# The order of the rows in W^T V, and who issues the first loads, in a fused low-rank FFN kernel

## The reference

```
base   = x @ W.T                                   # W: 1024 x 1024
logits = x @ Wr.T + 5.0 * one_hot(id)              # 8 experts
gates  = softmax over the top 2 of logits
h      = x @ A.T                                   # A: 8 experts x rank 16
lora   = (h * gates) @ B.T
out    = x + (base + 2.0 * lora) @ (U * S @ V.T).T # V: 1024 x 256, U: 1024 x 256
```

## Time and profile before

| | us |
|---|---|
| median of 3 runs | 157.66 |
| lowest, highest | 156.87, 158.06 |
| the profiled execution | 156.68 |
| its span, first to last instruction | 154.9 |
| busy TensorE, VectorE, ScalarE, GpSimd | 150.1, 103.1, 65.1, 70.1 |

### The profile page before, as it was taken

How to read it: one execution, slowest core, us unless ns; L and a number is a source line. 1 busy time by engine, 2 the same in 40 slices (tenths; PEclk the granted TensorE clock), 3 DMA queues, 4 the chain that set the end, 5 groups by cost and what they waited for, 6 DMA issues and landing times.

```text
span 154.9 us, 2559 instructions
## 1 busy us (share of the span) xinstructions
PE 150.1 (97%) x883; PEld 139.8 (90%) x883; DVE 103.1 (67%) x299; ACT 65.1 (42%) x147; POOL 70.1 (45%) x53
## 2 busy tenths in 40 slices
PE   7899999999999999999999999999999999999991
PEld 5799999999998999989998999899999989998880
DVE  0698697353658798765578476929692967396861
ACT  4696692519724642551155125414441642233200
POOL 2000024087764741259445935591669068701800
PEclk9999999999999999999999999999999999999999
DMA  5999999995303064148428744854680087006184
GB/s 184 326 395 395 405 418 405 408 402 204 135 7 130 4 271 135 80 154 310 136 99 312 268 135 180 287 215 135 261 259 25 0 292 252 2 22 253 70 333 141
DMA packets 10957, 32.72 MB, mean 211 GB/s; under 512 B 1472, under 2 KB 2496, under 8 KB 10816
## 3 DMA queue, kind: packets, MB, share of 16 engines
q1 hardware_dynamic: 10512, 31.96, 55.9%
q10 hardware_dynamic: 432, 0.59, 1.1%
HBM read 24.16 MB, written 8.39 MB: 210 GB/s over the span
## 4 chain that ended last, share of the span: by engine, by line
PE 93%; DMA 3%; DVE 1%; ACT 0%; ACTq 0%; issue 0%; DVEq 0%
PE pj L317 16%; PE pj L318 16%; PE pj L319 16%; PE fin L317 14%; PE fin L318 13%; PE fin L319 13%; DMA vw_raw<-in_VW 3%; PE zt L384 2%; PE gt L366 1%; PE zt L317 1%; PE zt L319 1%; PE zt L318 1%; DVE w_lo L702 0%; ACT w_hi L556 0%; DVE x_all L831 0%; ACTq L655 0%
## 5 line engine op out<-in xcount | busy, mean ns | idle before, releaser
L273 POOL TENSOR_TENSOR xT_lo<-xt_raw,xT_hi 128x1024 fp32r<-128x1024 f32 x16 | 40.5, 2532 | 55.1 <-ACT xT_hi L571 55.1
L317 PE MATMUL pj<-proj_hi,xT_hi 128*128 128x392 f32 x128 | 44.9, 351 | 0.0
L318 PE MATMUL pj<-proj_lo,xT_hi 128*128 128x392 f32 x128 | 43.5, 340 | 0.0
L319 PE MATMUL pj<-proj_hi,xT_lo 128*128 128x392 f32 x128 | 43.5, 340 | 0.0
L288 POOL TENSOR_TENSOR x_all<-x_all,vw_raw 128x512 f32<-128x512 f32 x18 | 23.0, 1295 | 17.5 <-DVE vw_raw L806 17.5
L317 PE MATMUL fin<-v_hi,w_hi 128*128 128x256 f32 (+1 forms) x84 | 26.9, 321 | 0.5 <-DVE w_lo L702 0.5
L318 PE MATMUL fin<-v_lo,w_hi 128*128 128x256 f32 (+1 forms) x84 | 26.3, 313 | 0.0
L319 PE MATMUL fin<-v_hi,w_lo 128*128 128x256 f32 (+1 forms) x84 | 26.3, 313 | 0.0
L317 PEld LDWEIGHTS pj<-proj_hi,xT_hi 128*128 128x128 f32 x128 | 24.0, 188 | 1.0
L318 PEld LDWEIGHTS pj<-proj_lo,xT_hi 128*128 128x128 f32 x128 | 24.1, 188 | 0.5
L319 PEld LDWEIGHTS pj<-proj_hi,xT_lo 128*128 128x128 f32 x128 | 24.0, 188 | 0.0
(11 more groups left out here) (87 smaller groups left out, 230.8 us busy)
## 6 DMA issues: line engine op xcount, KB each, us to landing
xt_raw<-in_xt SPq DMA_DIRECT2D x16, 512.0 KB, 3.6
x_all<-in_x SPq DMA_DIRECT2D x16, 512.0 KB, 5.7
out<-x_all SPq DMA_DIRECT2D x13, 512.0 KB, 2.7
w_raw<-in_W SPq DMA_DIRECT2D x8, 256.0 KB, 7.3
vw_raw<-in_VW SPq DMA_DIRECT2D x5, 384.0 KB, 6.8
out<-x_all SPq DMA_DIRECT2D x5, 256.0 KB, 2.0
u_raw<-in_U SPq DMA_DIRECT2D x1, 1024.0 KB, 13.0
vw_raw<-in_VW SPq DMA_DIRECT2D x3, 192.0 KB, 3.3
```

The lines of the kernel that those rows point to most:

```text
L273: nc.gpsimd.tensor_sub(xT_lo[:, t % 2, :, :], xt_raw[:, t % XTR, :, :], xT_hi[:, t % 2, :, :].bitcast(F32)).then_inc(xt_lo, 1)
L317: nc.tensor.matmul(dst, l_hi, r_hi, start=first, stop=False, skip_group_check=shared)
L318: nc.tensor.matmul(dst, l_hi, r_lo, start=False, stop=False, skip_group_check=shared)
L319: return nc.tensor.matmul(dst, l_lo, r_hi, start=False, stop=last, skip_group_check=shared)
```

## The change

The chunks of W^T V go by whole rows: chunk i is half h = i % 2 of row k = i // 2. V is split at every other chunk. SP issues both pieces of row 0, W[1], and then VW[k] and W[k] for k = 2 to 7, with ids, A|Wr, xt[0] and B between them. ScalarE issues nothing before its table load and its small exponential; after them it issues W[0] and VW[1]. The casts of A|Wr, x and B stand behind chunks 8, 10 and 12. All four banks become final in the last two chunks, and a new semaphore `p_ready` tells of them one by one; `split_p` for all four follows the last chunk. `step(0)` waits for one bank at every other k. TensorE makes 6 zero products instead of 7.

```diff
         def w_chunk(i):
-            return vw_raw[:, i, RANK:RANK + HQ] if i < OC else w_raw[:, i - OC, :]
+            return vw_raw[:, i // 2, RANK:RANK + HQ] if i % 2 == 0 else w_raw[:, i // 2, :]
...
             first = RANK + P
-            for k in range(3):
-                sp.dma_start(vw_raw[:, k, 0:first], VW[k, :, 0:first]).then_inc(vw_load[k], 16)
-            for k in range(3, OC):
+            sp.dma_start(vw_raw[:, 0, 0:first], VW[0, :, 0:first]).then_inc(vw_load[0], 16)
+            sp.dma_start(vw_raw[:, 0, first:], VW[0, :, first:]).then_inc(vw_rest_load, 16)
+            load_w(1)
+            for k in range(2, OC):
                 sp.dma_start(vw_raw[:, k, :], VW[k, :, :]).then_inc(vw_load[k], 16)
-            sp.dma_start(ids_i[:, :], ids).then_inc(ids_load, 16)
-            for k in range(OC):
                 load_w(k)
-            sp.dma_start(aw_raw[:, :, :], AW).then_inc(aw_load, 16)
-            load_xt(0)
-            sp.dma_start(b_raw[:, :, :], B).then_inc(b_load, 16)
+                if k == 2:
+                    sp.dma_start(ids_i[:, :], ids).then_inc(ids_load, 16)
+                if k == 4:
+                    sp.dma_start(aw_raw[:, :, :], AW).then_inc(aw_load, 16)
+                if k == 5:
+                    load_xt(0)
+                if k == 6:
+                    sp.dma_start(b_raw[:, :, :], B).then_inc(b_load, 16)
...
             def p_chunk(i):
-                h, k = divmod(i, OC)
+                k, h = divmod(i, 2)
...
+                    if k == OC - 1 and m % 2 == 1:
+                        last.then_inc(p_ready, 1)
+                if k < OC - 1:
+                    last.then_inc(w_used, 1)
...
                     if s == 0 and k == 0:
                         pe.wait_ge(aw_lo, 1)
-                        pe.wait_ge(p_lo, 2)
-                    if s == 0 and k in (MH, MH + 2):
+                    if s == 0 and k % 2 == 0:
                         pe.wait_ge(p_lo, k // 2 + 1)
...
-            for n in range(7):
+            for n in range(6):
...
             def split_p(b):
-                act.wait_ge(w_used, OC if b < 2 else 2 * OC)
+                act.wait_ge(p_ready, b + 1)
...
-            first = RANK + P
-            for k in range(3):
-                act.dma_start(vw_raw[:, k, first:], VW[k, :, first:]).then_inc(vw_rest_load[k], 16)
             act.wait_ge(const, 3 + E)
             nc.scalar.activation(esum[:, :], iota_e[:, 0:1], ACT.Exp).then_inc(act_warm, 1)
             act.wait_ge(act_warm, 1)
+            act.dma_start(w_raw[:, 0, :], W[0, :, :]).then_inc(w_load[0], 16)
+            act.dma_start(vw_raw[:, 1, :], VW[1, :, :]).then_inc(vw_load[1], 16)
             for i in range(2 * OC):
-                if i < OC:
-                    split_v(i)
+                if i % 2 == 0:
+                    split_v(i // 2)
                 split_w(i)
-                if i == OC + 4:
+                if i == OC:
                     act.wait_ge(aw_load, 16)
                     nc.scalar.copy(proj_hi[:, :, 0:Z0], aw_raw[:, :, :]).then_inc(aw_hi, 1)
-                if i == OC + 3:
-                    split_p(0)
-                    split_p(1)
-                if i == OC + 5:
+                if i == OC + 2:
                     split_x(0)
-                if i == OC + 6:
+                if i == OC + 4:
                     act.wait_ge(b_load, 16)
                     nc.scalar.copy(b_hi[:, :, :], b_raw[:, :, :]).then_inc(b_hi_done, 1)
-            split_p(2)
-            split_p(3)
+            for b in range(FINS):
+                split_p(b)
```

## The result

The changed kernel takes 160.37 us in the median of four runs (159.32 to 162.29), the kernel before 157.43; the ratio is 1.017, with a 95% interval of 1.012 to 1.022. A second set of runs gave 160.58 us and 1.020 (1.016 to 1.025). It is slower by 1.7 to 2.0%. The ratios leave out single runs that lie more than 1.5% above the fastest of their kernel, here the one of 162.29 us. The forecast was 158.6 us, 0.9 us up, with a chance of 0.66 for a change within 1% and 0.29 for slower by more than that.

The account below looks back on a forecast made before the run. The prediction took chunk 2's start, set by waits for the first loads, to bound the kernel. Its terms summed to +0.9 us, all at chunk 2, giving 158.6 us on the median, with a range of 156.8 to 160.4.

Parts of the forecast that it names:

- rival C: TensorE's clock stays or falls back low over chunks 1 and 2: +2.5 us, 160.2 us; chance 0.07.
- the main case: VW[1] lands late and delays chunk 2: +0.9 us, shift from -0.1 to +2.3, 157.5 to 160.0 us; chance 0.55.
- What sets the time: TensorE's start: no gap from chunk 2 at 8.57 us to step(0), so chunk 2's start sets the kernel's time.
- Issue times: ScalarE's queue: table load from 0.73 us, then W[0] issued at 2.27 and VW[1] at 2.7.
- Rival B: ScalarE's table load waits for iota_e until 1.9 us, both issues 1.2 us later: +2.1 us, 159.8 us; chance 0.08.
- Landing of W[0] and VW[1]: First loads: W[0] lands at 5.9 us, VW[1] at 7.8, within 6.7 to 9.1; chunk 2 at 9.5 instead of 8.57.
- the rate: First loads: bytes move at 375 GB/s, so the 1.84 MB taken for VW[1] are moved at 6.8 us.
- The equal share of the two queues: SP and ScalarE queues share the DMA engines about equally; middle counts 1.84 MB for VW[1], 1.12 MB for W[0].
- The lag: First loads: from bytes moved to landing takes 1.0 us, between 0.6 and 1.4.
- That W[0] decides nothing: Chunk 1 starts at 7.3 us and is over at 8.7, so VW[1] decides when chunk 2 starts.
- A zero product less: TensorE's start: chunk 0 at about 3.75 us instead of 4.14, worth 0.4 us there and nothing to chunk 2.
- A|Wr, x, B between chunks at no cost: Casts among the chunks cost 0 while the 1 us margin and stored chunks hold, even with a load 2 us later.

Follow-up runs that it names:

- e1_fill: Changed kernel with 14 products of zeros on TensorE between chunk 0 and chunk 1; 159.51 us, 1.012 of the kernel before.
- e1_again: The changed kernel with 14 zero products between chunks 0 and 1, run once more; 159.58 us, 1.014 of the kernel before.
- e3_act_first: Changed kernel with ScalarE's issues of W[0] and VW[1] ahead of its table load; 158.60 us, 1.004 of the kernel before.
- e7_before_6zeros: Kernel before with 6 zero products instead of 7 and nothing else; 157.40 us, 0.999 of the kernel before.
- e8_act_first_late: Changed kernel with ScalarE's two issues ahead of its table load, and A|Wr, x and B behind the rows; 158.46 us, 1.004 of the kernel before.
- e10_x_on_dve: Changed kernel, all loads on SP in use order, A|Wr behind row 5, x and B behind row 7, first x tile's low part on VectorE; 157.28 us, ratio 1.000.
- e2_sp_all: Changed kernel with W[0] and VW[1] issued by SP in order of use, ScalarE issuing nothing; 157.50 us, 0.9985 of the kernel before.
- e4_before_table: Kernel before with ScalarE's three pieces of rows 0 to 2 issued after its table load and small exponential; 162.50 us, 1.028 of the kernel before.
- a_again: The changed kernel itself, run once more; 160.58 us, 1.020 of the kernel before.
- e6_after_late: Changed kernel with loads and casts of A|Wr, x and B put back to the end of the rows; 161.87 us, 1.029 of the kernel before.
- e5_sp_all_late: Changed kernel with all loads on SP in use order, A|Wr, x, B loaded behind row 7, cast behind chunks 12 to 14; 157.37 us, ratio 1.000.

## Why the prediction was right or wrong

The measured 160.37 us lies at the upper edge of the range (160.4), and the likeliest time was 1.8 us short. That it lies inside is luck: the second set of runs gave 160.58, and this edge had been set by rivals B and C and the late end of the main case, none of which put the two loads as late as they came. Slower by over 1% had a chance of 0.29. Step by step:

- *What sets the time.* Right. Chunk 2 sets it: +3.88 us there, +3.97 at step(0), +4.0 at the end. That only what lies before chunk 2 counts held in every kernel that had neither a gap nor a slow clock behind it: step(0) came 20.2 to 20.3 us after chunk 2 in e1_fill, e1_again, e3_act_first, e7_before_6zeros, e8_act_first_late and e10_x_on_dve.
- *Issue times.* Right to 0.02 us. Rival B fell by the first row of ScalarE: the table load started at 0.74.
- *Landing of W[0] and VW[1].* The step that failed. Forecast 5.9 and 7.8, measured 8.3 and 9.8; even the late bound was 9.1. Of the 2.0 us by which VW[1] was missed, the rate made 0.7: by the GB/s of the windows from 1 us on, 1.84 MB are moved by about 7.5 us instead of 6.8. The equal share of the two queues made 0.4: loads landed in the order of their issue over both queues, so that not the middle but the upper counts hold, 1.97 MB for VW[1] and 1.31 MB for W[0], moved by 7.9 and 6.1. The lag made the rest: reckoned at 1.0 us from pairs of pieces that lay first in empty queues, it was 9.8 - 7.9 = 1.9 for VW[1] and 8.3 - 6.1 = 2.2 for W[0]. The kernel before had shown longer ones already: its third pair, 1.18 MB moved by 5.5, landed at 7.0, a lag of 1.5 that the prediction left out, and 1.97 MB issued had landed at 9.0. e2_sp_all, with the same loads issued third and fourth, and e4_before_table, with small pieces issued late, show that it is the late issue behind a backlog and neither the size nor the row order. The rule of the Trainium skill that stood beside the sum (DMA: Bandwidth & Descriptors, section "Issuing engines are not separate DMA queues") agrees: the loads of the two queues interleave, and issued 0.9 us earlier by ScalarE than by SP (e3_act_first, e2_sp_all) the same two landed 0.9 to 1.1 us earlier, and row 0's pieces later.
- *That W[0] decides nothing.* Wrong by the same term, and with it rival C. The idle time was reckoned as 1.4 us and was 3.2, and the clock fell. It was given a chance of 0.07 and priced at +1.6 over the main case; it cost 0.9 to 1.0 by e1_fill and e1_again. That 0.46 us idle had left the clock high was no evidence for a wait seven times that long. The two costs are not independent, as the prediction had them: late loads make the idle time that takes the clock.
- *A zero product less.* Right in both halves: chunk 0 at 3.71, and nothing won (e7_before_6zeros).
- *A|Wr, x, B between chunks at no cost.* Right for the changed kernel (TensorE has no gap from chunk 2 to step(0)), wrong in its reserve. "If a load came 2 us later, still 0" held only since all else was 4 us late: with chunk 2 at 8.3 in e2_sp_all TensorE lost 1.2 to 1.4 us before chunk 11, where x landed at 18.5 instead of the 16.5 reckoned and its cast stood in front of that of the chunk. What was missed besides is that VectorE is held for a whole GpSimd instruction; it was in the trace of the kernel before too, where three w_lo took 4.10 us from 21.91 on, beside GpSimd's subtraction from 22.22 to 24.86, with slack behind them.
- *split_p at the end.* Right: four casts from 30.83, step(0) without a wait.
- *The sum.* +0.9 forecast, +2.9 to +3.4 in the medians: of it 1.8 to 2.4 the loads and about 1.0 the clock. The direction and the place were right, the size was a third of the measured one.

## What to carry to other kernels

A load that is needed first must be issued first, counted over all queues. A second queue didn't let a load pass what another queue had issued before it: an issue 0.6 us later, fifth and seventh instead of third and fourth, meant a landing 3 us later. Price such a load from rows of loads that are issued behind a backlog, not from first pieces. And if a wait of the matmul engine at the start grows by microseconds, reckon the fall of its clock into the same case, not into another one.

## What the runs showed of the hardware

- The granted clock reads 1.00 in the rows before its first rise too, while matmuls of 256 columns are 0.21 us apart; only their distance tells the level. The first rise came by 4.5 us in one profile and at 9.3 in another, of two kernels whose first loads landed alike, worth 1.6 us.
- The clock fell in the four profiles in which TensorE idled for 3.2 to 4.4 us (the changed kernel, a_again, e6_after_late, e4_before_table), and not in those of e2_sp_all and e7_before_6zeros, with 1.2 and 1.8 us. In a_again it fell at 10.6, 0.4 us after TensorE had gone back to work.
- Loads landed in the order of their issue over both queues: in the five profiles with the changed kernel's first loads W[0], issued by ScalarE 0.15 us after SP's VW[2], landed within 0.3 us of it, in one of them before it.
- A DMA of 192 KB takes 2.4 us from issue to landing as the first of SP's queue alone, 2.7 to 2.9 beside a twin on ScalarE's queue, and 6.1 when issued 1.5 us later on that second queue, with 0.98 MB issued ahead of it.
- VectorE's subtraction of two SBUF operands is held while GpSimd's is under way: 2.64 us (e5_sp_all_late) and 2.47 (e2_sp_all) for 0.42 and 0.69, and no such case in e10_x_on_dve, where GpSimd does nothing in that stretch.
